# One kernel, two stages reordered: the second layer's projections and its attention

## What is computed

```python
# y: the stream, (2, 1024, 256)
lap_x = y[.., j-1] - 2*y[.., j] + y[.., j+1]          # over features, reflected
lap_y = the same over tokens
a = zX*lap_x + zY*lap_y + zR*y*(1 - y)
q, k = (a @ Wq.T, a @ Wk.T) in 8 heads of 32;  v = a @ Wv.T in 4 heads of 64
w = softmax(q*32**-0.5 @ k.T + causal mask)           # (2, 8, 1024, 1024)
diff = w[:, even heads] - lambda_full * w[:, odd heads]
attn = diff @ v                                       # then a norm, gamma, @ Wo.T
```

## Time and profile before

| | us |
|---|---|
| median of 3 runs | 1484.72 (1484.04 to 1485.09) |
| the profiled execution | 1482.76 |
| its span, first to last instruction | 1480.9 |
| PE busy | 1352.9 (91%) |
| DVE, ACT, POOL busy | 920.3 (62%), 760.9 (51%), 445.0 (30%) |
| projections block | 948.8 to 1012.2 |
| attention block, first score to last product | 1013.2 to 1258.1 |

### The profile page before, as it was taken

One profiled execution on the slowest core, in us unless ns is written; L12 is line 12 of the kernel. 1 busy time (PEld: TensorE's weight loads), 2 busy tenths in 40 slices (PEclk: granted clock), 3 DMA queues, 4 the chain that ended last, 5 costly groups with the idle time before them and its releaser, 6 DMA issues. The chain is left out here.

```text
span 1480.9 us, 25069 instructions
## 1 busy us (share of the span) xinstructions
PE 1352.9 (91%) x8742; PEld 1139.1 (77%) x8743; DVE 920.3 (62%) x1712; ACT 760.9 (51%) x1544; POOL 445.0 (30%) x450
## 2 busy tenths in 40 slices
PE   8999699888998789999999999798999899858998
PEld 3555366577975489999999999677788688638997
DVE  5977699765657843453343343386777777555676
ACT  4587867454222266555545555544555565234553
POOL 0000599420000261481090120024211200044885
PEclk9998899999998789999999999898999999978999
DMA  6000000100000131021010000050000000634550
GB/s 241 1 0 8 8 0 2 49 9 1 1 1 1 53 119 57 20 94 57 0 57 0 0 0 0 29 143 1 1 1 1 1 1 1 213 124 124 203 182 18
DMA packets 22894, 67.41 MB, mean 46 GB/s; under 512 B 4260, under 2 KB 8756, under 8 KB 18211
## 3 DMA queue, kind: packets, MB, share of 16 engines
q1 hardware_dynamic: 20514, 60.41, 11.8%
q0 software_dynamic: 2304, 6.03, 1.1%
HBM read 52.51 MB, written 14.19 MB: 45 GB/s over the span
## 5 line engine op out<-in xcount | busy, mean ns | idle before, releaser
L1886 DVE TENSOR_TENSOR ehidl<-hT,ehidh 128x512 fp32r<-128x512 f32 x148 | 132.7, 905 | 140.5 <-ACT ehidh L1869 139.8
L1863 ACT ACTIVATE hT<-ps,eb 128x256 f32<-128x256 f32 x296 | 124.4, 472 | 165.0 <-PE ps L1694 165.0
L2396 ACT ACTIVATE pr<-ps,nmax 128x256 f32<-128x256 f32 (+7 forms) x128 | 94.0, 739 | 103.0 <-DVE nmax L2426 102.9
L1694 PE MATMUL ps<-kh,qz 128*128 128x512 f32 (+3 forms) x384 | 125.1, 380 | 5.8 <-DVE maskb L2410 3.6
L1893 DVE SCALAR_TENSOR_TENSOR X<-ps,wE,X 128x256 f32 x74 | 35.9, 485 | 111.3 <-PE ps L1694 101.8
L1869 ACT CAST ehidh<-hT 128x512 fp32r<-128x512 f32 x148 | 91.9, 621 | 4.7
L2426 DVE TENSOR_REDUCE nmax<-ps 128x1 f32<-128x256 f32 (+7 forms) x128 | 91.1, 749 | 1.2 <-PE ps L2336 0.6
L1694 PEld LDWEIGHTS ps<-kh,qz 128*128 128x128 f32 x384 | 76.2, 199 | 15.8 <-ACT pr L2396 4.8
L1694 PE MATMUL ps<-hTh,ew_0h 128*128 x288 | 82.1, 285 | 5.4 <-issue 5.4
L1694 PE MATMUL ps<-hTh,ew_1h 128*128 x304 | 85.4, 281 | 0.0
L1694 PE MATMUL ps<-ew_1h,ehidh 128*128 128x256 f32 x304 | 85.0, 280 | 0.4 <-POOL ew_1l L1806 0.4
(11 more groups left out here) (546 smaller groups left out, 4218.8 us busy)
## 6 DMA issues: line engine op xcount, KB each, us to landing
ew1s<-in_ew_dram SPq DMA_DIRECT2D x8, 1024.0 KB, 4.7
ew2s<-in_ew_dram SPq DMA_DIRECT2D x8, 1024.0 KB, 6.7
fw1s<-in_fw_dram SPq DMA_DIRECT2D x8, 1024.0 KB, 7.7
fw2s<-in_fw_dram SPq DMA_DIRECT2D x8, 1024.0 KB, 9.5
slot_rows<-fill SPq DMA_DIRECT2D x1, 5140.0 KB, 21.0
xr<-slot_rows SPq DMA_DIRECT2D x8, 514.0 KB, 4.2
xT<-in_xT_dram SPq DMA_DIRECT2D x4, 512.0 KB, 7.3
X<-in_x_dram SPq DMA_DIRECT2D x1, 2048.0 KB, 18.1
```

Of the source, the lines that this page charges most:

```text
L1694: last = nc.tensor.matmul(out, lhs[a], rhs[b], start=(start and n == 0), stop=(stop and n == 2), **kw)
L1863: nc.scalar.activation(hid[:, f, :], ps[:, f // 2, (f % 2) * JOB:(f % 2 + 1) * JOB], ACT.Gelu, bias=b1[q][:, f:f + 1]).then_inc(k.e_act, 1)
L1886: nc.vector.tensor_tensor(lo[:, f, :], hid[:, f, :], hi[:, f, :], ALU.subtract).then_inc(k.e_lo, 1)
L2396: nc.scalar.activation(pr[:, n % 3, u, 0:wide], half(n, u, wide), ACT.Exp, bias=nmax[:, n % 2, u:u + 1], accum_out=sums[:, u, n:n + 1]).th ...
```

## The change

In the attention each engine's queue is permuted: PE issues scores before transposes and takes the products three units back instead of two; ACT does the exponentials before its copies; DVE takes the maxima before the difference, and `collect` moves from after a tile's third unit (one tile back) to ahead of a tile's first (two tiles back). In the projections the queues of PE, ACT and DVE are permuted, and the three `low_weight` go from POOL to DVE. No instruction is added or dropped.

```diff
 # laplace_phase, tensor queue
             turn(1, 1)
+            turn(2, 0)
+            turn(2, 1)
+            turn(3, 0)
+            turn(3, 1)
             second_difference(0, 0)
             second_difference(0, 1)
-            turn(2, 0)
-            turn(2, 1)
+            keys(0, 0)
             second_difference(1, 0)
-            keys(0, 0)
+            second_difference(1, 1)
             keys(0, 1)
+            second_difference(2, 0)
+            second_difference(2, 1)
             values(0, 0)
-            turn(3, 0)
-            turn(3, 1)
-            second_difference(1, 1)
-            second_difference(2, 0)
+            keys(1, 0)
+            queries(0, 0)
             values(0, 1)
...
 # scalar queue
-            high_weight(0)
+            operator()
             stream(0, 0)
             high(0, 0)
             stream(0, 1)
...
             stream(1, 0)
             high(0, 1)
             stream(1, 1)
-            operator()
             growth(1)
+            high(1, 0)
+            high_weight(0)
+            high_derivative(0, 0)
+            high_derivative(0, 1)
+            stream(2, 0)
+            stream(2, 1)
             high_weight(2)
-            high(1, 0)
             high(1, 1)
+            high_keys(0, 0)
+            high(2, 0)
+            high(2, 1)
+            stream(3, 0)
+            growth(2)
             high_weight(1)
...
 # gpsimd queue
-            low_weight(0)
-            low_weight(2)
-            low_weight(1)
             clear(0)
...
 # vector queue
+            def low_weight(n):
+                dve.wait_ge(k.l_wh, ROUND.index(n) + 1)
+                nc.vector.tensor_tensor(PARTS[n][1][:, :, :], WHOLE[n][:, :, :], PARTS[n][0][:, :, :],
+                                        ALU.subtract).then_inc(k.l_wl, 1)
+
...
             differences(0, 1)
+            low_derivative(0, 0)
+            low_weight(0)
             low(1, 0)
             growth(1)
+            low_derivative(0, 1)
             low(1, 1)
-            low_derivative(0, 0)
-            low_derivative(0, 1)
             neighbours(1)
+            differences(1, 0)
+            differences(1, 1)
+            low(2, 0)
+            low(2, 1)
             low_keys(0, 0)
-            differences(1, 0)
-            low(2, 0)
-            low_keys(0, 1)
-            low(2, 1)
-            growth(2)
-            differences(1, 1)
-            low(3, 0)
-            low(3, 1)
+            low_weight(2)
             low_derivative(1, 0)
             low_derivative(1, 1)
+            low_weight(1)
+            low_keys(0, 1)
+            growth(2)
+            low(3, 0)
             neighbours(2)
...
 # attention_phase, tensor queue
-            for n in range(UNITS + 2):
-                if n >= 2:
-                    turn(n - 2)
+            for n in range(UNITS + 3):
                 if n < UNITS:
                     scores(n, 0)
                     scores(n, 1)
-                if n >= 2:
-                    product(n - 2)
+                if 2 <= n < UNITS + 2:
+                    turn(n - 2)
+                if n >= 3:
+                    product(n - 3)
 # scalar queue
             for n in range(UNITS + 2):
-                if n >= 2:
-                    turn(n - 2)
                 if n < UNITS:
                     exponentials(n, 0)
                     exponentials(n, 1)
+                if n >= 2:
+                    turn(n - 2)
 # vector queue
             for n in range(UNITS):
+                if n % HEADS == 0 and n >= 2 * HEADS:
+                    collect(n // HEADS - 2)
+                largest(n, 0)
+                largest(n, 1)
                 if n:
                     difference(n - 1)
-                largest(n, 0)
-                largest(n, 1)
-                if n % HEADS == 2 and n > 2:
-                    collect(n // HEADS - 1)
             difference(UNITS - 1)
+            collect(NT - 2)
             collect(NT - 1)
```

More of the change, by code:

```diff
@@ L2072, in _ @@
             stream(1, 1)
-            operator()
             growth(1)
+            high(1, 0)
[4 more added lines that the diff above has]
+            stream(2, 1)
             high_weight(2)
-            high(1, 0)
             high(1, 1)
-            high_weight(1)
[L2079 to L2085, removed]
+            high_keys(0, 0)
[3 more added lines that the diff above has]
+            growth(2)
+            high_weight(1)
+            stream(3, 1)
+            high_derivative(1, 0)
+            high_derivative(1, 1)
             high_keys(0, 1)
-            growth(2)
-            stream(3, 0)
-            stream(3, 1)
+            growth(3)
+            high(3, 0)
             values(0, 0)
[L2091 to L2094, removed]
             values(0, 1)
             high_keys(1, 0)
-            growth(3)
+            high(3, 1)
+            high_queries(0, 0)
+            high_derivative(2, 0)
             high_keys(1, 1)
-            high_derivative(2, 0)
             high_derivative(2, 1)
+            values(1, 0)
             high_keys(2, 0)
-            values(1, 0)
-            high_queries(0, 0)
+            values(1, 1)
             high_keys(2, 1)
+            high_queries(0, 1)
             high_derivative(3, 0)
+            high_queries(1, 0)
+            values(2, 0)
             high_derivative(3, 1)
-            values(1, 1)
+            values(2, 1)
             high_keys(3, 0)
-            values(2, 0)
             high_keys(3, 1)
-            high_queries(0, 1)
-            high_queries(1, 0)
-            values(2, 1)
+            values(3, 0)
             high_queries(1, 1)
+            values(3, 1)
             high_queries(2, 0)
-            values(3, 0)
             high_queries(2, 1)
-            values(3, 1)
             high_queries(3, 0)
@@ L2212, in _ @@
             differences(0, 1)
+            low_derivative(0, 0)
+            low_weight(0)
             low(1, 0)
             growth(1)
+            low_derivative(0, 1)
             low(1, 1)
-            low_derivative(0, 0)
-            low_derivative(0, 1)
             neighbours(1)
+            differences(1, 0)
+            differences(1, 1)
+            low(2, 0)
+            low(2, 1)
             low_keys(0, 0)
-            differences(1, 0)
-            low(2, 0)
-            low_keys(0, 1)
-            low(2, 1)
-            growth(2)
-            differences(1, 1)
-            low(3, 0)
-            low(3, 1)
+            low_weight(2)
             low_derivative(1, 0)
             low_derivative(1, 1)
+            low_weight(1)
+            low_keys(0, 1)
+            growth(2)
+            low(3, 0)
             neighbours(2)
+            differences(2, 0)
             low_keys(1, 0)
-            differences(2, 0)
+            differences(2, 1)
+            low(3, 1)
+            low_derivative(2, 0)
+            low_keys(1, 1)
+            low_derivative(2, 1)
             growth(3)
-            differences(2, 1)
-            low_derivative(2, 0)
-            low_derivative(2, 1)
-            low_keys(1, 1)
+            low_queries(0, 0)
             neighbours(3)
```

26 lines of the change are left out of this document (9 added, 17 removed).

## The result

The changed kernel takes 1465.0 us (median of 4 runs, 1460.05 to 1467.77) against 1484.9 for the kernel before on the same chip (4 runs, 1484.04 to 1487.03): ratio 0.9855, interval [0.9837, 0.9873]. That is 19.9 us faster by the medians, 18.9 to 24.2 by the interval. The forecast was 1458.7, 26 us faster. The profiled execution is one of 1465.69 us.

A forecast was written before the change was run, and what follows sets the result against it. PE was taken as the only engine near full, with a DVE-ACT ring stalling the attention. Attention 20 us less and projections 6 less give 1456.8 in the profiled execution, 1458.7 on the median; range 1450 to 1472.

The forecast's parts named there:

- DVE's sleep goes: Attention: the 0.92 us DVE slept per four-block unit for ACT's exponentials goes; PE's period becomes 2.9 to 3.0 us.
- The sum for the attention, 225: Attention: 215 us of PE work plus 5, 4, 0.5 and 1 us of additions, 20 us less than before.
- Term (a): Attention's start: 10 us at 1.2 GHz as before, where PE needs more time than DVE; adds 5 us.
- term (b): Second batch's one- and two-block units: DVE's excess over PE and some 4 us of low clock; adds 4 us.
- delay 1.0 us, inside the slack: Attention, each tile's start: collect ahead of the first maximum delays it 1.0 us, within five-block units' slack of 1 us.
- Projections, -6: Second layer's projections: block ends 6 us earlier, POOL and DVE together; bounds 8 and 2 us.
- The price of 1.8 us on DVE: Projections: three 128x512 low-weight subtractions in DVE's queue add 1.8 us there.
- A: Attention: queueing on a nearly full DVE keeps half of the 30 us of stalls; attention 235, total 1469.7 us; chance 0.14.
- B: Attention: POOL's placement copies exclude DVE for whole instructions; +11 us, total 1470; chance 0.06.
- C: Projections give nothing: the six-microsecond hole brings a second clock drop and DVE is last; total 1464.7 us; chance 0.08.
- D: Attention slower: clock stays at 1.2 GHz through units of one to four blocks in both batches; about 1501 us; chance 0.04.
- E: No clock loss: 5 us of (a), 1 of (b) and 2 in the projections come back; 1451 us; chance 0.04.

The follow-up runs named there:

- warm: Changed kernel plus sixteen 128x512 matmuls on PE behind the last query projection, keeping PE busy until the attention: 1463.83 us, 0.9837 of the kernel before.
- spread: Changed kernel with POOL's clears not waiting for the last low derivative and each tile's collect cut into three pieces over its first three units: 1459.96 us.
- collect_later: Changed kernel with DVE's whole collect moved behind the difference in a tile's first unit: 1463.22 us, 0.9832 of the kernel before.
- clears_early: Changed kernel with POOL's second and third clear right behind the zero fill, not waiting for the last low derivative: 1461.93 us, 0.9821 of the kernel before.
- weights_pool: Changed kernel with the three low weights back on POOL, behind the clears and the zero fill: 1467.59 us, 0.9874 of the kernel before.
- noplace: Changed kernel with POOL's query placements from the fourth tile on replaced by one-column copies: 1461.57 us, 0.9836 of the kernel before.
- two_back: Changed kernel with PE's products two units back, behind their transposes, instead of three: 1654.7 us, 1.1116 of the kernel before.
- dve_only: Kernel before with only DVE's new attention order; PE, ACT and the projections old: 1562.42 us, 1.0516 of the kernel before.

## Why the prediction was right, and where its sizes were off

- **DVE's sleep goes; PE's period is 2.9 to 3.0.** Right: no such wait is left and the period is 2.94.
- **The sum for the attention, 225, measured 226.8.** Close, but by luck in part, since terms missed in opposite ways. Term (a), 5 us for the low clock: it was low for the 10 us foreseen, as this window of after shows (clock is the third value from the end), but `warm` took 3.5 of them away and gained only 0.7 us. The instruction times double, yet in the small units DVE needs almost the same time, so PE waits for it at either clock. At that rate the term was 2 us, at the rate of the second batch's stretch (1.4 us for 3.4) it was 4; both are extrapolations. And the 4 us of low clock that term (b) took "as today", for about 2 us, did not come in the trace of after; where they came they cost 1.4.

```profile
1013.28:1023.00 9.72, 9.72 (x52) 9.49 (x52) 5.89 (x26) 5.87 (x24) 2.79 (x8) 0.52 0.01 2
1023.00:1241.00 218.00, 211.25 (x1519) 184.22 (x1518) 181.45 (x360) 134.24 (x332) 44.43 (x97) 1.00 0.00 1
```

- **The collect, "delay 1.0 us, inside the slack".** Wrong in size: the holes are 7.4 us, part of which term (b) already held as DVE's excess in small units. They offset what (a) and (b) had too much of. The step that failed can be read at the first unit of a four-block tile, PE's mask of the first half and DVE's instructions:

```profile
1037.41 0.23 PE L2336 MATMUL ps<-maskb,identb 128*128 128x128 bf16 x1
```

```profile
1037.54 0.17 DVE L2442 RECIPROCAL rc<-sums 128x4 f32<-128x4 f32 x1
...
1039.11 1.29 DVE L2426 TENSOR_REDUCE nmax<-ps 128x1 f32<-128x512 f32 x2
```

  I counted the delay from the end of both halves' scores. But DVE begins with the first half, whose mask ends at 1037.64, 0.1 us after the collect began: the whole 1.57 us are delay. Less the slack of 1.0 that I had worked out for five blocks, that leaves 0.6, and 0.6 is what the first five-block units lost. `spread` got 3.4 us back, `collect_later` none.
- **Projections, -6 measured -2.8 (-3.5 as the mean of the traces).** The early part was right to a few tenths, counted from the block's start: first copy 0.7 (0.8 forecast), second differences of window 0 5.9 (5.8), first keys 14.1 (13.8), with the forecast hole before them (4.60 us instead of 6.3). From there each step was late. Half clock after the hole lasted 5.3 us (966.03 to 971.3), not 3, and DVE waited 1.49 and 0.49 for the second differences made in it; PE's second keys ended 1.3 us late (21.3 against 20.0) and its last query 1.7 (56.9 against 55.2); the dense part in between was sized right. What failed is the last step: I put the last low derivative 3.6 us earlier by shifting it with PE, without walking DVE's queue, which had three more subtractions in it and waited for ACT (0.87 in the row above). It began at 45.5, only half a microsecond earlier than before, and POOL's 3.63 and 10.6 us, both sized right, hang on it. `clears_early` shows it: with that wait gone, the same PE and DVE queues give 59.5, the 58.8 forecast within 0.7. Most of the 2.8 us that did come is a gain that the prediction did not name as one: it added clears and placements without a gap, where the kernel before has 2.30 us of waiting between them.
- **DVE or POOL for the low weights.** The price of 1.8 us on DVE was right (3 x 0.6), and the alternative is worse (`weights_pool`).
- **Rivals.** A (queueing) holds in part: the holes behind each collect are such queueing, but the attention is 226.8 and not 235, and PE's waits on `L2345` are 4.3 us in small units, not in wide ones as it said. B (POOL excludes DVE, 11 us) is refuted in size for the placements: about 2 us in `noplace`, the bound that the prediction had itself set from its rows, and the mean difference of 640 columns takes 0.93 us in both traces, of 1024 columns 1.31. C (projections give nothing) lies about as far from what happened (-2.8 to -3.6) as the forecast (-6) does: the hole did bring half clock, and DVE's queue held up the chain that ends the block. D is refuted for the changed kernel: the clock is 1.00 from 1023 to the attention's end, above. A low clock that stays does occur, in `two_back` and `dve_only`. E (no loss to clock) is not what happened either: the clock fell, and cost less than the forecast had.

One thing the prediction held true and never tested was that the queues could be reasoned about one at a time. The gain is that of all three: DVE's order alone costs 77 us, PE's and ACT's alone 19, and without ACT's there is no gain. My expectations for `dve_only` and `two_back` made the same error, by 90 us and by 130 or more: they priced an instruction that waits, not the circle that it closes, nor the low clock that stands beside such a circle. In `two_back` the waits alone are 95.0 us where 30 to 60 had been expected, and PE's longer busy time is another 104.

## What to carry to other kernels

When a pipeline is written out as one fixed queue per engine, write down for each engine pair whose step must precede whose, with the unit numbers, and follow every circle until it closes; its length is the period, and a queue permuted alone can close one that holds every engine. Expect to lose more than the waits: in the two kernels with a pause of PE in nearly every unit the clock was at half for 80 and 230 us of the attention. Cut work that comes once per tile into pieces of the size of a unit's slack rather than look for a better place for the lump. And before forecasting that a block ends earlier because its busiest engine does, walk the chain that ends it on the other engines too, here a wait of POOL's that `clears_early` leaves out. And read the clock in both traces before taking a difference of 1 or 2 us between two stages for the effect of an edit.

## What the runs showed of the hardware that was not expected

**The clock fell while PE was working.** In `warm` PE stood still for 0.77 and for 0.44 us between 1007 and 1014.3, no longer, and yet ran at half clock from 1014.24, busy 6.36 of 6.60 us. What went before the fall were sixteen matmuls of 512 columns at full clock until 1011.2, and then 2.3 us of one-block units, whose matmuls have 128. Which of the two, short stops or small matmuls, brings it down no run here tells apart. And it was down for long in the two kernels whose PE pauses in nearly every unit: some 230 of 419 us in `two_back` and 80 of 324 in `dve_only`, against 9 of 227 in after.

**DVE and POOL held each other, in one place a lot and in another hardly.** Besides the subtractions of `weights_pool`, a DVE operation on two columns waited there beside POOL's clearing of a buffer; it takes 0.17 us when POOL is still:

```profile
949.92 1.85 POOL L2126 MEMSET qz<- 128x1024 f32 x2 [87.14 <-POOLq L3099]
```

```profile
949.97 1.82 DVE L2153 TENSOR_SCALAR zc<-rows 128x2 f32<-128x2 f32 x1 [1.78 <-PEq L3099]
```

In the attention of after the placement copies lost more than DVE:

```profile
1063.45 2.34 POOL L2265 CAST qz<-ql 32x256 fp32r<-32x256 f32 x4
```

```profile
1063.01 1.07 DVE L2436 SCALAR_TENSOR_TENSOR pr<-pr,rr 128x640 f32<-128x640 f32 x1
```

Four copies took 2.34 us instead of 1.70, the difference 1.07 instead of 0.88. The Trainium skill (SBUF — State Buffer, "SBUF: two separate sides") has one of the two take the shared ports for a whole instruction while the other blocks, in the cases that it names. The rows of subtractions and differences fit that; whether the operation on two columns is such a case no run shows. Beside a subtraction DVE loses up to the rest of that instruction (1.26 us when POOL is alone), beside a placement copy less than the 0.43 of one. It is not always one instruction: the 1.82 us of the operation on two columns reach over two clearing instructions of 0.93 each, while in after the same operation took 0.93 beside such a pair. Rival B's price was wrong rather than the rule: it charged DVE with every copy, and the difference lost 0.19 us. That each such wait is the lock and nothing else was not tested apart.
